# The statistics of chunks 2 and 3 computed, turned, stored and spread at earlier places of one fused attention and feed-forward kernel

## The chip, the cores and the metric
The kernel runs on one core of one Trainium2 chip. The metric is the device time of one execution in microseconds (us); lower is better. The engines of the core named here are TensorE (matrix products and turns), VectorE, ScalarE, GpSimd (three small jobs only) and SyncE (issues nearly all transfers). In the rows they are PE (PEld for its weight loads), DVE, ACT, POOL and SP; a queue of an engine, which issues its transfers, has a q behind the name (SPq).

## What is computed
```python
xn = _layernorm(x, axis=-1)
x = x + attn(xn) + ffn(xn)
# attn: x_norm = layernorm(xn) * gamma + beta; q, k, v = x_norm @ qkv
#       softmax(causal(q k^T * scale)) @ v @ o_proj + xn
# ffn:  h = silu(xn @ w_gate) * (xn @ w_up), of each 4 values the 2 largest kept; h @ w_down
```
x is 2048 rows of 512 values, float32; q, k and v are 512 wide, the hidden layer 2048.

## The kernel before
The 2048 rows are 16 tiles of 128 rows and 4 chunks (0 to 3) of 4 tiles. Every float32 operand of a product is split into a high and a low half, and a product is three matmuls: high by high, high by low, low by high. So a result in PSUM is cast to the high half by ScalarE and then subtracted to the low half by VectorE, which also frees the bank. q and k are never made: the weights are multiplied beforehand, a chunk's z (`zg`) is the transposed chunk by the joint weight, and scores are x by z. In the same way v and the output projection are one weight.

The order of the work is one hand-written list, `steps`. Each engine runs through the same list and emits what it has to do for a step, so a step's place in the list sets its place in the program of each engine, and in SyncE's queue too. An engine takes its instructions strictly in order; what waits holds all that stands behind it. Semaphores order the engines among each other.

The steps that the change moves, for a chunk c:

- `stat[c]` (four) and `x_stats[c]`: VectorE reads the four tiles of x in `xw` (L1510) and joins the sums to mean and variance (L1514).
- `x_rstd[c]`: GpSimd adds and raises to -0.5 (L686, L687, L690).
- `x_scale[c]`: four small VectorE instructions (L1520 to L1523) make the columns of scale and shift, `row_stat`.
- `row_turn[c]`: TensorE turns these columns into rows (L763); `row_copy[c]`: VectorE copies them out of the bank (L1562).
- `row_store[c]`: SyncE stores them to memory (L552); `row_spread[c]`: SyncE waits for that store and loads them back over all 128 partitions, 1 MB, as `spread` (L558).
- `xt_load[c]`: SyncE loads x transposed, 2 transfers of 512 KB (L493). For chunk 2 the destination is where chunk 1's spread lies, so it waits until `xn[1]` has read that.

What uses them: `xh_pre[c][k]` (VectorE, L1541 and L1543) scales the transposed chunk, a quarter k at a time, with `spread` and gamma; `xh[c][k]` rounds it to the high half (ScalarE, L1168) and takes the low half (VectorE, L1565). `z_round[c][k]` are TensorE's products for z (L840, 48 matmuls for a chunk). `xn[c]` (L1549, L1551) applies the first normalization to the same transposed data for the feed-forward part, `xn_store[c]` stores it.

Chunk 0 is attended tile by tile (`head`, `scores`, `attend`, `rows`). Chunks 1 to 3 are done in wide units: `unit[c]` is a list of scores of 128 keys against all 512 rows of the chunk (TensorE L699 to L701, ScalarE's copy L1202, VectorE's maximum L1436 to L1448); then the maximum over the partitions (GpSimd, L693), the softmax in parts (`shift`, `exp_wide`, `split`, `meet`) and the rows. `v[c]` are the four products of V (L699 to L701), their bank is needed again by z of the next chunk. In unit lists of chunk 1, `v[1]` and then z of chunk 2 follow the units; in those of chunk 2, z of chunk 3 follows them. `block_sum` makes four sums of blocks for the feed-forward part and stores them.

The list around the change, before:
```python
between = {3: [*z_round[1][1:4], *z[1]]}
steps += [*u[0:2], ("rows_store", OLD - 1, 0), *stat[2], x_stats[2], x_rstd[2], xn[1][0], x_scale[2], xn[1][1], xn_store[1], xt_load[2], u[2],
          row_turn[2], row_copy[2], row_store[2], u[3], row_spread[2], ...
```
SyncE's waits for these steps:
```python
elif n == 2: sp.wait_ge(xn_ready[1], 2)          # xt_load
else:        sp.wait_ge(stats_ready, NCH)        # xt_load of chunk 3
sp.wait_ge(row_stat_stored, 16 * n)              # row_spread
if n == 3: sp.wait_ge(sums_turned, 1)            # row_spread of chunk 3, over chunk 1's maxima and sums
```

Of the kernel before, what the change touches and what calls it, by code (L numbers as in the profile page):

```python
# [28 lines left out]
def attention_ffn(nc, x, x_t, qkv_t, o_proj, gamma, beta, w_units, w_down, out):  # L29
# [3 lines left out]
    NCH = S // W  # L33
    TC = W // P
# [21 lines left out]
    def fills(kind, n):  # L56
        return [(kind, n, k) for k in range(KT)]
# [4 lines left out]
    xh_pre, xh, z, z_round, v = ([fills(kind, c) for c in range(NCH)] for kind in ("xh_pre", "xh", "z", "z_round", "v"))  # L62
    x_stats, x_rstd, x_scale, row_turn, row_copy, xw_load, row_store, row_spread, xt_load, xn_store = (
        [(kind, c, 0) for c in range(NCH)] for kind in ("x_stats", "x_rstd", "x_scale", "row_turn", "row_copy", "xw_load", "row_store",
                                                        "row_spread", "xt_load", "xn_store"))
    stat = [fills("stat", c) for c in range(NCH)]
    xn = [fills("xn", c)[0:2] for c in range(NCH)]
# [3 lines left out]
    steps = [step for k in range(3) for step in (hi[0][k], hi[1][k], lo[0][k], lo[1][k], qk_round[k])]  # L71
# [6 lines left out]
    steps += [*vo, *stat[1][0:2], *z[0], *stat[1][2:4], x_stats[1], x_rstd[1], xw_load[3], v[0][0],  # L78
              ("scores", 0, 0), exp[0], x_scale[1], row_copy[1], v[0][1], row_turn[1], row_store[1], row_spread[1]]
    before = {3: [z_round[1][0]]}  # L80
    between = {3: [*z_round[1][1:4], *z[1]]}
    beside = {0: [v[0][2]],
              1: [xh_pre[1][0], v[0][3], xh[1][0]],
              2: [xh_pre[1][1], xh_pre[1][2], xh[1][1], xh_pre[1][3], xh[1][2], xh[1][3]]}

# [1 line left out]
    OLD = TC * WIDE[0]  # L87
# [15 lines left out]
    def wide_parts(c):  # L103

        own = TC * c
        return [(0,), (1,), *((u, u + 1) for u in range(2, own + TC, 2))]
# [5 lines left out]
    def softmax(c, after, behind):  # L112

        last = len(wide_parts(c)) - 1
        order = [shift[c][0], exp_wide[c][0], *after.get(-1, []), shift[c][1], split[c][0], *after.get(0, []), shift[c][2], exp_wide[c][1]]
        for j in range(1, last + 1):
            if j == 3:
                order += meet[c][0:3]
            order += [*exp_wide[c][j + 1:j + 2], split[c][j], *after.get(j, []), *shift[c][j + 2:j + 3], *behind.get(j, []), *(meet[c][j:j + 1] if j >= 3 else [])]
        return order  # L120

    rows_of = {c: [[("rows", n, 0), ("rows_store", n, 0)] for n in range(TC * c, TC * (c + 1))] for c in WIDE}
    u = unit[1]
    steps += [*u[0:2], ("rows_store", OLD - 1, 0), *stat[2], x_stats[2], x_rstd[2], xn[1][0], x_scale[2], xn[1][1], xn_store[1], xt_load[2], u[2],
              row_turn[2], row_copy[2], row_store[2], u[3], row_spread[2], *u[4:6], xh_pre[2][0], u[6], xh_pre[2][1], u[7], ("max_fold", 1, 0), ("max_all", 1, 0),
              ("rows_load", OLD + 1, 0), xh[2][0], v[1][0], xh_pre[2][2], xh[2][1], v[1][1], xh_pre[2][3], xh[2][2], v[1][2], xh[2][3], v[1][3], *z_round[2]]
    steps += softmax(1, {}, {2: [*z[2], *xn[0], xn_store[0]], 4: [("block_sum", 0, 0)]})
    steps += [("sum_turn", 1, 0), *rows_of[1][0], *rows_of[1][1], ("rows_load", OLD + 2, 0), ("rows_load", OLD + 3, 0), *stat[3], x_stats[3], x_rstd[3], xt_load[3]]
    u = unit[2]
    steps += [*u[0:3], *rows_of[1][2], x_scale[3], *rows_of[1][3], ("rows_load", OLD + 4, 0), ("rows_load", OLD + 5, 0), u[3],  # L130
              row_turn[3], row_copy[3], row_store[3], row_spread[3], xn[2][0],
              *u[4:6], xn[2][1], xn_store[2], u[6], xh_pre[3][0], u[7], xh_pre[3][1], xh[3][0], u[8], xh_pre[3][2], xh[3][1], u[9],
              xh_pre[3][3], xh[3][2], *u[10:], ("max_fold", 2, 0), ("max_all", 2, 0), xh[3][3], *z_round[3], *z[3][0:2]]
    steps += softmax(2, {-1: [z[3][2]], 0: [z[3][3]], 1: v[2][0:2], 2: v[2][2:4]}, {4: [xn[3][0]], 5: [xn[3][1], xn_store[3]]})
# [1 line left out]
    u = unit[3]  # L136
# [60 lines left out]
    with ExitStack() as ctx:  # L197
        def sem(name):
            return ctx.enter_context(nc.semaphore(name))
# [4 lines left out]
        def at(name, offset, shape, dt):  # L204
            return nc.alloc_sbuf_tensor_at(name, shape, dt, offset=base + offset)
# [8 lines left out]
        def products_ahead(no):  # L214
# [10 lines left out]
                  for c, pair in enumerate(((112, 116), (208, 212), (24, 28), (120, 124)))]  # L225
# [18 lines left out]
                           for name, cols, dt in (("own_raw", OWN_W + P, F32), ("own_lo", OWN_W, F32R)))  # L244
# [4 lines left out]
        sum_pair, max_all = ({c: at(f"{name}{c}", o[c - WIDE[0]] * KB, shape, F32) for c in WIDE}  # L249
                             for name, o, shape in (("sum_pair", (88, 136, 168), [P, 2, W]), ("max_all", (94, 92, 172), [P, W])))  # L250
# [83 lines left out]
        max_ready, exp_ready, group_attended, rows_ready = sem("max_ready"), sem("exp_ready"), sem("group_attended"), sem("rows_ready")  # L334
# [361 lines left out]
        def _(pe):  # L696
# [51 lines left out]
            def row_bank_free(no):  # L748

                if no < TURN_RING:  # L750
                    pe.wait_ge(prod_free, 2 * KT)

            def turn_rows(n):

                c = 0 if n == 1 else n
                no = turn_no["row_turn", n]
                if no >= TURN_RING:
                    pe.wait_ge(turn_free, no - TURN_RING + 1)
                row_bank_free(no)
                if n == NCH - 1:  # L760
                    pe.wait_ge(rows_ready, TC * (n - 1))
                pe.wait_ge(scale_ready, n + 1)
                pe.transpose(turn_bank[no % TURN_RING][0:(n + 1 - c) * 4 * TC, 0:P], row_stat[:, c:n + 1, :, :, :].rearrange("p c v t o -> p (c v t o)"),  # L763
                             ident[:]).then_inc(turn_full, 1)
# [139 lines left out]
            for kind, n, k in steps:  # L904
# [4 lines left out]
                elif kind == "z_round":  # L909
                    z_round(n, k)  # L910
                elif kind == "row_turn":
                    turn_rows(n)
                elif kind == "x_turn":

# [29 lines left out]
                elif kind == "meet":  # L944
                    u = wide_parts(n)[k][-1]
# [957 lines left out]
```

## Time and profile before
| | |
|---|---|
| median of 3 runs | 803.7 us (800.33 to 805.3) |
| the profiled execution | 802.0 us |
| its span, first to last instruction | 800.2 us |
| TensorE busy | 788.8 us (99%) |
| VectorE busy | 610.8 us (76%) |
| ScalarE busy | 319.6 us (40%) |
| GpSimd busy | 18.9 us (2%) |
| mean granted TensorE clock | 0.994 |

The span is the part of the execution that the profile covers, and 1.8 us lie around it. Busy time of TensorE is a modelled figure: matmuls overlap, and one of 512 columns is shown with 0.39 us while the next starts 0.227 us after it. So distances between starts tell more than busy shares. The granted clock is the share of full speed that TensorE was given; full speed is 2.4 GHz, and 0.50 is the lower of its two levels, 1.2 GHz.

### The profile page before, as it was taken

The numbers are of one execution on the slowest core, as the hardware profiler recorded it, in microseconds if no ns is written. First come the engines' busy times: TensorE is split into PE (matmuls) and PEld (weight loads), VectorE is DVE, ScalarE is ACT, GpSimd is POOL, SyncE is SP. The second block draws the span as 40 slices with busy tenths as digits, with TensorE's granted clock in tenths as the row PEclk, the third lists the DMA queues.
The fourth block names the chain that finished last, engine by engine and source line by source line (L and its number), as shares of the span: only waits on it lengthen the run. The fifth ranks groups of instructions, "written<-read, shape, count | busy, mean of one in ns | idle before, by whom it ended". The sixth has DMA issues, their size and how long they took to land.

```text
span 800.2 us, 9296 instructions
## 1 busy us (share of the span) xinstructions
PE 788.8 (99%) x3518; PEld 651.7 (81%) x3518; DVE 610.8 (76%) x964; ACT 319.6 (40%) x514; POOL 18.9 (2%) x26
## 2 busy tenths in 40 slices
PE   9999979989999999999999999999999999999998
PEld 6888858878888888888888888888888888888887
DVE  7978497775824688779989889799559558559786
ACT  5423142124312354564636436364334334335441
POOL 2010110101000000000000000000000000000000
PEclk9999989999999999999999999999999999999999
DMA  9441501730022325587426435497467262261002
GB/s 325 174 169 44 185 0 61 255 106 1 27 79 79 109 102 220 174 325 280 185 73 266 188 79 210 180 348 291 154 214 262 102 235 92 95 236 54 0 1 106
DMA packets 31611, 121.74 MB, mean 152 GB/s; under 512 B 3088, under 2 KB 3664, under 8 KB 29136
## 3 DMA queue, kind: packets, MB, share of 16 engines
q1 hardware_dynamic: 30272, 119.00, 40.4%
q10 hardware_dynamic: 1296, 2.16, 0.8%
q8 instruction: 28, 0.46, 0.2%
q14 instruction: 15, 0.12, 0.0%
HBM read 77.07 MB, written 44.07 MB: 151 GB/s over the span
## 4 chain that ended last, share of the span: by engine, by line
PE 78%; DMA 2%; DVE 1%; issue 0%; ACT 0%; SPq 0%; DVEq 0%
PE bank L960 13%; PE bank L961 13%; PE bank L962 13%; PE bank L1040 7%; PE bank L1042 7%; PE bank L1041 7%; PE bank L701 5%; PE bank L699 5%; PE bank L700 5%; PE bank L840 2%; DMA spread<-row_stats 1%; DMA resid<-rows 0%; DMA row_stats<-rows_turned_t 0%; DVE xh_raw L1541 0%; DVE xh_raw L1543 0%
## 5 line engine op out<-in xcount | busy, mean ns | idle before, releaser
L960 PE MATMUL bank<-X_hi,wset 128*128 128x512 f32 x448 | 174.4, 389 | 0.0
L962 PE MATMUL bank<-X_hi,wset 128*128 128x512 f32 x448 | 174.3, 389 | 0.0
L961 PE MATMUL bank<-X_lo,wset 128*128 128x512 f32 x448 | 174.3, 389 | 0.0
L960 PEld LDWEIGHTS bank<-X_hi,wset 128*128 128x128 f32 x448 | 84.1, 188 | 17.6 <-issue 0.2
L962 PEld LDWEIGHTS bank<-X_hi,wset 128*128 128x128 f32 x448 | 84.1, 188 | 17.5
L961 PEld LDWEIGHTS bank<-X_lo,wset 128*128 128x128 f32 x448 | 84.1, 188 | 17.4
L1040 PE MATMUL bank<-dw,hs_hi 128*128 128x512 f32 x224 | 87.2, 389 | 0.0
L1042 PE MATMUL bank<-dw,hs_lo 128*128 128x512 f32 x224 | 87.1, 389 | 0.0
L1041 PE MATMUL bank<-dw,hs_hi 128*128 128x512 f32 x224 | 87.1, 389 | 0.0
L1674 DVE TENSOR_TENSOR acc<-bank,acc 128x512 f32<-128x512 f32 x59 | 40.1, 687 | 40.0 <-PE bank L1042 39.6
L699 PE MATMUL bank<-zg,xT 128*128 128x512 f32 (+2 forms) x132 | 49.8, 377 | 0.0
L701 PE MATMUL bank<-zg,xT 128*128 128x512 f32 (+2 forms) x132 | 49.5, 375 | 0.0
L700 PE MATMUL bank<-zg,xT 128*128 128x512 f32 (+2 forms) x132 | 49.4, 375 | 0.0
L1040 PEld LDWEIGHTS bank<-dw,hs_hi 128*128 128x128 f32 x224 | 42.1, 188 | 8.9 <-DVE acc L1674 0.2
L1042 PEld LDWEIGHTS bank<-dw,hs_lo 128*128 128x128 f32 x224 | 42.1, 188 | 8.8
L1041 PEld LDWEIGHTS bank<-dw,hs_hi 128*128 128x128 f32 x224 | 42.0, 188 | 8.7
L699 PE MATMUL bank<-v_hi,wide_hi 128*128 128x512 f32 x126 | 49.0, 389 | 0.0
L700 PE MATMUL bank<-v_lo,wide_hi 128*128 128x512 f32 x126 | 49.0, 389 | 0.0
L840 PE MATMUL bank<-xT,mu_hi 128*128 128x512 f32 x128 | 38.9, 420 | 7.4 <-DVE v_lo L1575 5.0
L1221 ACT COPY g_sum<-bank 128x512 f32<-128x512 f32 x32 | 18.9, 589 | 56.5 <-PE bank L962 56.5
L840 PEld LDWEIGHTS bank<-xT,mu_hi 128*128 128x128 f32 x128 | 25.9, 203 | 14.7 <-DVE v_lo L1575 6.3
L1202 ACT COPY wide_raw<-bank 128x512 f32<-128x512 f32 x20 | 11.8, 588 | 58.6 <-PE bank L701 58.6
(259 smaller groups left out, 1441.7 us busy)
## 6 DMA issues: line engine op xcount, KB each, us to landing
w_operands<-wset SPq DMA_DIRECT2D x8, 3584.0 KB, 13.5
wset<-w_operands SPq DMA_DIRECT2D x8, 3584.0 KB, 12.5
wsum<-w_units SPq DMA_DIRECT2D x28, 256.0 KB, 3.8
dw_raw<-L_ffn_w_down SPq DMA_DIRECT2D x14, 512.0 KB, 5.4
xw<-L_attn_x SPq DMA_DIRECT2D x4, 1024.0 KB, 9.6
xt_raw<-x_t SPq DMA_DIRECT2D x8, 512.0 KB, 7.5
xn_t<-xt_raw SPq DMA_DIRECT2D x8, 512.0 KB, 2.8
acc<-resid SPq DMA_DIRECT2D x2, 2048.0 KB, 9.8
```

Source lines behind the costliest of these rows:

```text
L699: pe.matmul(dst, l_hi, r_hi, start=(n == 0 and flags.get("first", True)), stop=False)
L700: pe.matmul(dst, l_hi, r_lo, start=False, stop=False)
L701: last = pe.matmul(dst, l_lo, r_hi, start=False, stop=(n == len(pairs) - 1 and flags.get("last", True)))
L840: return pe.matmul(product_bank(no)[:], lhs[left][:, q, m * P:(m + 1) * P], rhs[right][:, q, :], start=first, stop=(q == KT - 1 and right ...
L960: pe.matmul(dst[:], u[:, 0, :], x_hi, start=(first and kt == 0), stop=False, skip_group_check=True)
L961: pe.matmul(dst[:], u[:, 0, :], x_lo, start=False, stop=False, skip_group_check=True)
L962: last = pe.matmul(dst[:], u[:, 1, :], x_hi, start=False, stop=(kt == 1), skip_group_check=True)
L1040: pe.matmul(dst, s_hi, d_h, start=(r == 0 and i != ND - 2), stop=False)
L1041: pe.matmul(dst, s_hi, d_l, start=False, stop=False)
L1042: last = pe.matmul(dst, s_lo, d_h, start=False, stop=(r == G - 1 and i != ND - 3))
L1221: nc.scalar.copy(dst[:], src[:]).then_inc(kept[m], 1)
L1674: nc.vector.tensor_tensor(acc[:, tile, :], down_bank(i, t)[:], acc[:, tile, :], ALU.add).then_inc(added, 1)
```

## The change
The statistics of chunk 2 go into the attention of chunk 0: two of them ahead of V's third tile, the other two with the sums and GpSimd's step ahead of z of chunk 1, and the scale behind `z[1]`. Chunk 2's turn, copy, store and spread open the part of chunk 1, ahead of its first wide unit and of the load of x transposed. The whole statistics of chunk 3, which stood behind chunk 1's softmax, with the load of chunk 3's transposed x, go into the first units of chunk 1; its turn, copy and store follow unit 4, and its spread stands behind chunk 1's turned sums, ahead of all stores and loads of rows. The last wait of TensorE for rows ahead of chunk 3's turn is gone. The scalings of chunk 2 (`xh_pre[2]`) and its low halves stand one to two steps earlier among units 5 to 7, and ahead of V.
```diff
-    between = {3: [*z_round[1][1:4], *z[1]]}
-    beside = {0: [v[0][2]],
+    between = {3: [*stat[2][2:4], x_stats[2], x_rstd[2], *z_round[1][1:4], *z[1], x_scale[2]]}
+    beside = {0: [*stat[2][0:2], v[0][2]],
...
-    steps += [*u[0:2], ("rows_store", OLD - 1, 0), *stat[2], x_stats[2], x_rstd[2], xn[1][0], x_scale[2], xn[1][1], xn_store[1], xt_load[2], u[2],
-              row_turn[2], row_copy[2], row_store[2], u[3], row_spread[2], *u[4:6], xh_pre[2][0], u[6], xh_pre[2][1], u[7], ("max_fold", 1, 0), ("max_all", 1, 0),
-              ("rows_load", OLD + 1, 0), xh[2][0], v[1][0], xh_pre[2][2], xh[2][1], v[1][1], xh_pre[2][3], xh[2][2], v[1][2], xh[2][3], v[1][3], *z_round[2]]
+    steps += [row_turn[2], row_copy[2], row_store[2], row_spread[2], *u[0:2], ("rows_store", OLD - 1, 0), *xn[1], xt_load[2], xn_store[1],
+              *stat[3], x_stats[3], x_rstd[3], xt_load[3], *u[2:4], x_scale[3], u[4], row_turn[3], row_copy[3], row_store[3], xh_pre[2][0], u[5],
+              xh_pre[2][1], xh[2][0], u[6], xh_pre[2][2], xh[2][1], u[7], ("max_fold", 1, 0), ("max_all", 1, 0), ("rows_load", OLD + 1, 0),
+              xh_pre[2][3], xh[2][2], v[1][0], xh[2][3], *v[1][1:4], *z_round[2]]
...
-    steps += [("sum_turn", 1, 0), *rows_of[1][0], *rows_of[1][1], ("rows_load", OLD + 2, 0), ("rows_load", OLD + 3, 0), *stat[3], x_stats[3], x_rstd[3], xt_load[3]]
+    steps += [("sum_turn", 1, 0), row_spread[3], *rows_of[1][0], *rows_of[1][1], ("rows_load", OLD + 2, 0), ("rows_load", OLD + 3, 0)]
...
-    steps += [*u[0:3], *rows_of[1][2], x_scale[3], *rows_of[1][3], ("rows_load", OLD + 4, 0), ("rows_load", OLD + 5, 0), u[3],
-              row_turn[3], row_copy[3], row_store[3], row_spread[3], xn[2][0],
+    steps += [*u[0:2], *rows_of[1][2], *rows_of[1][3], ("rows_load", OLD + 4, 0), ("rows_load", OLD + 5, 0), *u[2:4], xn[2][0],
...
-                if n == NCH - 1:
-                    pe.wait_ge(rows_ready, TC * (n - 1))
```
SyncE's queue behind the spread of chunk 1, before. `xn_t` with `xt_raw_0_52` and `_1_53` is chunk 1's normalized store, `xt_raw_0_54` and `_1_55` chunk 2's transposed x, `spread_111` chunk 2's spread.
```order
L565 DMA xn_t<-xt_raw_0_52 128x2x512
L565 DMA xn_t<-xt_raw_1_53 128x2x512
L493 DMA xt_raw_0_54<-x_t 128x2x512
L493 DMA xt_raw_1_55<-x_t 128x2x512
L552 DMA row_stats<-rows_turned_t 16x128
L558 DMA spread_111<-row_stats 128x2048
L565 DMA xn_t<-xt_raw_0_50 128x2x512
```
The same place of SyncE's queue with the change; `xt_raw_0_56` and `_1_57` are chunk 3's.
```order
L552 DMA row_stats<-rows_turned_t 16x128
L558 DMA spread_111<-row_stats 128x2048
L493 DMA xt_raw_0_54<-x_t 128x2x512
L493 DMA xt_raw_1_55<-x_t 128x2x512
L565 DMA xn_t<-xt_raw_0_52 128x2x512
L565 DMA xn_t<-xt_raw_1_53 128x2x512
L493 DMA xt_raw_0_56<-x_t 128x2x512
L493 DMA xt_raw_1_57<-x_t 128x2x512
L552 DMA row_stats<-rows_turned_t 16x128
```
Store and spread of chunk 2 have gone from last to first; chunk 3's transposed x and store have come in.

VectorE from the low half of z of chunk 1 (`zg`) to the maximum of unit 4 (the first with `own_raw_86`), before:
```order
L1575 TENSOR_TENSOR zg<-bank,zg 128x512 x4
L1382 TENSOR_SCALAR rows<-rows,one_rstd,neg_mean_rstd 128x512
L1389 SCALAR_TENSOR_TENSOR rows<-bank,inv_sum,rows 128x512
L1510 BN_STATS stats<-xw_80 128x6 x4
L1514 BN_AGGR mean_var<-stats 128x2 x4
L1549 TENSOR_TENSOR xt_raw_0_52<-xt_raw_0_52,spread_110 128x1024
L1551 TENSOR_TENSOR xt_raw_0_52<-xt_raw_0_52,spread_110 128x1024
L1520 SCALAR_TENSOR_TENSOR row_stat<-mean_var,row_stat 128x4
```
VectorE from the same `zg` with the change (line numbers are 2 lower there):
```order
L1573 TENSOR_TENSOR zg<-bank,zg 128x512 x4
L1518 SCALAR_TENSOR_TENSOR row_stat<-mean_var,row_stat 128x4
L1519 TENSOR_SCALAR one_rstd<-row_stat 128x4
L1520 SCALAR_TENSOR_TENSOR neg_mean_rstd<-mean_var,row_stat 128x4
L1521 SCALAR_TENSOR_TENSOR row_stat<-mean_var,row_stat 128x4
L1380 TENSOR_SCALAR rows<-rows,one_rstd,neg_mean_rstd 128x512
L1387 SCALAR_TENSOR_TENSOR rows<-bank,inv_sum,rows 128x512
L1560 COPY rows_turned_t<-bank 16x128
L1547 TENSOR_TENSOR xt_raw_0_52<-xt_raw_0_52,spread_110 128x1024
```
The scale of chunk 2 has come right behind `zg`, and the copy of the turned rows stands ahead of the normalized copy of chunk 1.

VectorE behind the maximum of unit 4 with the change; before, the first scaling (L1541 there) stood behind the maximum of unit 5.
```order
L1446 TENSOR_TENSOR max_pair_95<-max_pair_95,own_raw_86 128x512
L1560 COPY rows_turned_t<-bank 16x128
L1539 SCALAR_TENSOR_TENSOR xh_raw_60<-xt_raw_0_54,gamma_t,spread_111 128x512
L1541 SCALAR_TENSOR_TENSOR xh_raw_60<-spread_111,gamma_t,xh_raw_60 128x512
L1444 TENSOR_TENSOR own_raw_86<-own_raw_86,causal_t 128x128
```
The copy of chunk 3's turned rows now stands just ahead of chunk 2's first scaling.

## Rows read from the trace of the kernel before

**Rows 1.** Waits of PE: line waited for, us in total, times, longest us
```profile
PE bank L840 <- DVE v_lo L1575: 5.0, 3, 2.3
PE bank L840 <- ACT own_raw L1202: 2.4, 1, 2.4
```
**Rows 2.** Windows: stretch, busy time of each engine, clock, DMA share, GB/s
```profile
61.60:73.00 11.40, 11.40 (x54) 9.40 (x53) 9.18 (x15) 4.91 (x9) 0.00 (x0) 1.00 0.14 48
...
105.20:124.90 19.70, 14.69 (x50) 11.08 (x50) 16.34 (x25) 9.33 (x14) 0.89 (x1) 0.83 0.00 0
172.10:187.70 15.60, 13.16 (x51) 10.36 (x51) 9.79 (x19) 3.60 (x8) 2.19 (x1) 0.89 0.00 0
```
**Rows 3.** Timeline of PE, z of chunk 2: start, length, instruction, idle before
```profile
105.23 0.42 PE L840 MATMUL bank<-xT,mu_hi 128*128 128x512 f32 x1
...
111.96 0.79 PE L840 MATMUL bank<-xT,mu_hi 128*128 128x512 f32 x1 [0.47 <-DVE v_lo L1575]
...
124.86 0.39 PE L699 MATMUL bank<-v_hi,wide_hi 128*128 128x512 f32 x1
```
**Rows 4.** Timeline of PE, first wide unit of chunk 2 and z of chunk 3
```profile
142.91 0.48 PE L699 MATMUL bank<-zg,xT 128*128 128x512 f32 x1
...
172.19 0.90 PE L840 MATMUL bank<-xT,mu_hi 128*128 128x512 f32 x2
175.52 1.22 PE L840 MATMUL bank<-xT,mu_hi 128*128 128x512 f32 x2 [2.43 <-ACT own_raw L1202]
...
187.68 0.39 PE L699 MATMUL bank<-vo_hi,xT 128*128 128x512 f32 x1
```
**Rows 5.** Timeline of SPq, store and spread of chunk 2
```profile
88.43 0.50 SPq L552 DMA_DIRECT2D row_stats<-rows_turned_t  x1
93.85 0.35 SPq L558 DMA_DIRECT2D spread<-row_stats  x1
```
**Rows 6.** Line L552, the three stores of turned statistics
```profile
DMA to landing us min/median/max: 1.6/2.4/5.4
```
**Rows 7.** Timeline of DVE: unit 4, first scaling of chunk 2, last low half of V
```profile
91.02 0.69 DVE L1448 TENSOR_TENSOR max_pair<-max_pair,own_raw 128x512 f32<-128x512 f32 x1
...
98.53 0.75 DVE L1541 SCALAR_TENSOR_TENSOR xh_raw<-xt_raw,gamma_t,spread 128x512 f32<-128x512 f32 x1 [4.96 <-DMA spread<-row_stats]
...
111.22 0.69 DVE L1575 TENSOR_TENSOR v_lo<-bank,v_hi 128x512 fp32r<-128x512 f32 x1
```
**Rows 8.** The chain that ended last, from 60 to 175: start, us, what
```profile
160.37 6.83 DMA spread<-row_stats
```
**Rows 9.** Timeline of DVE: low half of V's third tile, zg, statistics
```profile
50.18 0.69 DVE L1575 TENSOR_TENSOR v_lo<-bank,v_hi 128x512 fp32r<-128x512 f32 x1 [2.16 <-ACT v_hi L1182]
...
71.77 2.73 DVE L1575 TENSOR_TENSOR zg<-bank,zg 128x512 fp32r<-128x512 f32 x4 [1.89 <-ACT zg L1182]
...
76.67 2.46 DVE L1510 BATCH_NORM_STATS2 stats<-xw 128x6 f32<-128x512 f32 x4
```
**Rows 10.** Timeline of POOL, the steps for chunks 1 and 2
```profile
41.76 0.23 POOL L686 TENSOR_SCALAR radicand<-mean_var 128x4 f32<-128x4 f32 x1 [23.67 <-DVE mean_var L1514]
...
79.64 1.11 POOL L686 TENSOR_SCALAR radicand<-mean_var 128x4 f32<-128x4 f32 x1 [35.62 <-DVE mean_var L1514]
...
82.06 1.67 POOL L690 TENSOR_TENSOR row_stat<-radicand,neg_half 128x8 f32<-128x8 f32 x1
```
**Rows 11.** Line L493, the eight loads of x transposed
```profile
DMA to landing us min/median/max: 5.3/7.5/12.8
```
**Rows 12.** Groups of instructions from 100 to 125: busy us, mean ns
```profile
L1182 ACT CAST v_hi<-bank 128x512 fp32r<-128x512 f32 x4 | 2.3, 568 | 0.0
```
**Rows 13.** Timeline of DVE: zg of chunk 2, low half of part 3
```profile
123.64 2.73 DVE L1575 TENSOR_TENSOR zg<-bank,zg 128x512 fp32r<-128x512 f32 x4 [0.85 <-ACT zg L1182]
...
132.34 1.09 DVE L1633 TENSOR_TENSOR own_lo<-own_raw,wide_hi 128x896 fp32r<-128x896 f32 x1
```
**Rows 14.** DMA issues: KB each, median us to landing
```profile
rows<-L_attn_x SPq DMA_DIRECT2D x10, 256.0 KB, 2.7
```

## The prediction

> **What bounds the kernel now.** I read the waits of TensorE first, over the whole span. Beside the start there are two: 5.0 us for the low halves of V and 2.4 us for a ScalarE copy, both at line 840, the products z of a chunk [rows 1]. So TensorE sets the time, and a gain can only come from these two places. The windows around them give their full size, since a slowed clock comes on top of the idle time: from 61.6 to 73.0, where z of chunk 1 lies, 54 matmuls take 11.4 us at clock 1.00; the two others have 0.83 and 0.89 [rows 2]. The timeline of TensorE gives the lengths. 48 full matmuls 0.227 us apart, as they stand at full clock, make an undisturbed z 10.9 us long (the 54 hold the same 48 and some narrow ones, 11.4). **Stall A**, z of chunk 2, starts at 105.23 and is followed by other work at 124.86: 19.6 us, so 8.7 us lost [rows 3]. **Stall B**, z of chunk 3, runs from 172.19 to 187.68: 15.5 us, 4.6 us lost [rows 4]. Together 13.3 us; all else in the rows is TensorE's own work.
>
> Why A: on SyncE's queue the store of chunk 2's turned statistics stands behind two loads of x transposed. It is issued at 88.43, and the spread that needs it at 93.85 [rows 5]: 5.4 us, where these stores took 1.6, 2.4 and 5.4 us [rows 6]. The Trainium skill ("DMA: Bandwidth & Descriptors", section on queues, rings and completion order) says that an engine consumes descriptors of a ring in order; these rows agree. The spread lands at 98.5, ending 5.0 us of idle time on VectorE, and from there VectorE works without a gap of note until the last low half of V at 111.91 [rows 7]; only then does TensorE get its last bank (111.96) [rows 3]. Why B: the chain goes through chunk 3's spread, issued at 160.37, 6.8 us on its way, to the scaling at 167.2 [rows 8].
>
> **The change, part by part.** Nothing is added: the same 8 statistics, turns, stores and spreads, minus one TensorE wait.
>
> (1) Two statistics of chunk 2 go ahead of V's third tile of chunk 0, where VectorE stood idle for 2.16 us; they take 0.65 us each and cost nothing. The other two and the four sums (1.6 us) go where it stood idle for 1.89 us before zg [rows 9]. Hidden, with 0.2 to 0.3 us to spare; uncovered, zg and with it the first wide unit of chunk 1 come up to 1.6 us later.
>
> (2) Chunk 2's scale now waits for GpSimd between zg and the last rows, and TensorE turns it before the first wide unit, at 75.7. Statistics end near 71.5. GpSimd's three steps took 4.1 us from 79.64 to 83.73; with the first two as short as the 0.23 us at 41.76 they make 2.3 [rows 10]: ready at 73.8 or 75.6, the scale 0.3 us later than the end of zg (74.4) or than 75.6. TensorE waits 0 or 0.3 us, against 0.4 us lost at the turn near 84 now. I take no change, between 0.3 gained and 0.3 lost.
> The first step took 1.11 us beside VectorE's normalized copy, which has two operands in SBUF, and 0.23 us at 41.76 [rows 10]. The Trainium skill ("SBUF — State Buffer", section on the two separate sides) has GpSimd and VectorE lock a shared port pair when VectorE has two SBUF inputs. Zg has one in PSUM, so by the rule the short price holds and the sum is 0.3 us better than by the long one; no row here decides it.
>
> (3) Copy, store and spread of chunk 2: rows of tile 3 end near 77.0, the copy at 77.3. Store 1.6 to 2.4 us, spread 4.7 (93.85 to 98.5) to 6.8 us [rows 5 to 8]: in place between 83.8 and 86.7, no longer last.
>
> (4) What is last then? VectorE does chunk 1's normalized copy (4.9 us, now in one piece, to 82.2), then chunk 3's statistics (2.8 us, to 85.1), which hide in its old idle time. x transposed for chunk 2 is loaded from 82.2, landing 5.3 to 7.5 us later, the least and the median of these loads [rows 11]: 87.5 to 89.7. The wide units' maxima keep their place in TensorE's rhythm. The one of unit 4 ends near 91.6 [rows 7]; the copy of chunk 3's statistics behind it takes 0.3 us, so chunk 2's first scaling starts at 91.9 instead of 98.5: 6.6 us earlier. From 98.53 to 111.91 VectorE needs 13.4 us [rows 7]; the maximum of unit 5, done before 98.5 now, comes inside: 0.9 us. VectorE's bound for the end of V's last low half is 91.9 + 14.3 = 106.2.
> TensorE's own bound is later: V's last matmul starts 0.23 us before 105.23 and lasts 0.39, ScalarE's cast takes 0.57, the low half 0.69: 106.7 [rows 3, 7, 12]. The fourth bank of z is wanted at 105.23 + 3 × 0.227 = 105.9, so 0.8 us of stall A stays, and VectorE has 0.5 us to spare. **A gains 8.7 − 0.8 = 7.9 us.** I take it that 0.8 us leaves the clock alone: the 2.4 us wait ahead of 175.52 brought it down, and the 46 matmuls behind it took 12.2 instead of 10.4 us [rows 2, 4]. That price, 1.7 us, is the other bound.
>
> (5) The softmax behind it. VectorE starts the shifts 5.2 us earlier (106.65 for 111.82), TensorE ends z 7.9 us earlier; so what slack it has shrinks by 2.7 us. The tightest place is the low half of part 3: VectorE made it at 132.34 + 1.0 = 133.4, TensorE used it at 124.86 + 48 × 0.227 = 135.7 [rows 3, 13]. Slack 2.4 us, minus 2.7, plus what ScalarE's wait for TensorE before zg gives back: VectorE stood idle for 0.85 us there [rows 13]. About 0.4 us is left. I take no stall; the other bound is 2.7 − 2.4 = 0.3 us, and later parts have more slack.
>
> (6) Stall B. TensorE reaches chunk 2's wide units at 135.0 (142.9 now) and z of chunk 3 at 164.2 [rows 4]. Chunk 3's store was long ago; its spread is issued behind the four block sums and the turned sums, near 135.5, and lands by 142.3 even at 6.8 us [rows 8]. Chunk 3's scaling now goes by VectorE's program order: the second half of chunk 2's copy ends near 156.1, the first scaling at 157.6, with three maxima, two more scalings and one low half the third is done at 163.6, ScalarE's activation at 164.3 and its copies of units 10 and 11 at 164.7 and 165.0. TensorE wants these banks at 164.6 and 164.9. So 0.3 us stays of 4.6. **B gains 4.3 us**, between 2.5 us (VectorE 1.8 us late) and 4.6.
>
> (7) Chunk 3's turn costs TensorE 0.2 us before and after alike. Its old wait for rows held nobody. Behind z of chunk 3 everything hangs on TensorE, which does not wait again [rows 1], and moves as a whole.
>
> **Sum**: 7.9 + 4.3 = 12.2 us. The profiled execution took 802.0 us (span 800.2), which gives 789.8; against the median of the runs, 803.7, it is 791.5. I forecast 790.5.
>
> **The rivals.**
> *The load of x transposed comes late* (0.10). It shares the queue with the spread, 1 MB, just ahead. At 12.8 us, the longest of these loads [rows 11], it lands at 95.0: VectorE starts 3.1 us late, 0.5 of them free; A gains 5.3, with some clock lost 4.5. 794. Against it: the 12.8 us belong to the start, with 16 loads queued.
> *The softmax of chunk 1 becomes the bound* (0.08). If my 0.4 us of slack is 1 to 2 us too high, TensorE waits before part 3, and that much comes back: 792 to 793.
> *Rows stand behind the spread* (0.07). SyncE's queue now holds the 1 MB spread ahead of the stores and loads of rows 4 to 7, and VectorE cannot go on to maxima without rows 6 and 7. They are wanted by 146.5. The store of rows 4 lands with the spread at 142, the load takes 2.7 us more [rows 14], 145 to 146 with rows 7: just hidden. If it is 3 us later, B keeps its stall with the clock: 795.
> *Nothing to be had* (0.04): the banks of V hold z up whatever VectorE does, A keeps its 8.7 us, only B gains: 799. Against it: VectorE, not ScalarE, released every matmul at A.
> *Slower than before* (0.03). The same head of the queue: the spread waits for chunk 1's turned sums, and everything of SyncE behind it waits with it. Each us by which rows 6 land after 147 costs VectorE one and TensorE one; past 159 the whole gain is gone, at 165 it is 808 us. This needs 20 us for a store and a load of 256 KB each, and such a load takes 2.7 [rows 14].
>
> **How the numbers follow.** The forecast has 0.68: 790.5, with its own bounds of 788.5 (no clock, no leftovers) to 793.5 (clock lost at A, B at 2.5). Rivals one to three reach to 795, four to 799. The base itself lies between 800.3 and 805.3. The range 786.5 to 797.5 leaves out rivals four and five and the ends. What a measurement of this kernel can tell from no change is about 1%, 8 us: the forecast and most of rivals one and two are beyond it, 0.80; part of rivals one to three and rival four within, 0.17; slower 0.03.
>
> **What would show it.** Right: z of chunk 2 ends 11.5 to 12 us after it starts, one wait of 0.7 us at its fourth matmul; z of chunk 3 in 11.2 us; clock 1.00 in both; VectorE's wait for the spreads is gone, and the first scaling of chunk 2 starts near 92 right behind the copy. Wrong: a wait of VectorE for x transposed ahead of that scaling; TensorE waiting for a low half before part 3; VectorE idle for rows near 143; or clock below 1.00 at 106 to 110.

## The result and the profile after

The changed kernel takes 789.9 us (median of 4 runs, 789.6 to 790.2), the kernel before, on the same chip, 802.0 (800.3 to 805.3): a ratio of 0.984, 95% interval 0.981 to 0.986. The forecast was 790.5. The profiled execution took 789.8 us (span 788.0), 12.2 us less than that of before, which is the sum worked out above. Two executions far from all others (1610 us, one of 20 of the kernel before in the first group of experiments, and 1129 us, one of 5 of the last experiment) are left out of the ratios and ranges.

TensorE's waits, as in [rows 1]:
```profile
PE bank L897 <- DVE warm L1478: 1.0, 1, 1.0
PE bank L838 <- DVE v_lo L1573: 0.5, 1, 0.5
```
Of the 5.0 us at chunk 2's z, 0.5 is left, and the 2.4 us at chunk 3's z is gone. (The first row is the start of the program and stood in the kernel before too; a third one, 0.2 us, is also at the start, at 13.66.) The windows, as in [rows 2], over z of chunks 1, 2 and 3:
```profile
61.60:73.00 11.40, 11.40 (x54) 9.44 (x53) 10.72 (x22) 4.61 (x8) 0.66 (x3) 1.00 0.15 47
105.50:117.40 11.90, 11.42 (x49) 8.94 (x48) 9.15 (x14) 7.11 (x11) 0.00 (x0) 1.00 0.00 0
164.50:175.50 11.00, 11.00 (x49) 8.94 (x49) 6.82 (x15) 2.55 (x6) 2.20 (x1) 1.00 0.00 0
```
The first number behind the stretch is its length; the clock is the third from the end. It was 0.83 and 0.89 in the two lower ones [rows 2] and is 1.00 in both. The timeline of TensorE has the lengths, against [rows 3, 4]:
```profile
62.22 1.07 PE L838 MATMUL bank<-xT,mu_hi 128*128 128x512 f32 x4
...
105.51 1.08 PE L838 MATMUL bank<-xT,mu_hi 128*128 128x512 f32 x3
107.07 0.50 PE L838 MATMUL bank<-xT,mu_hi 128*128 128x512 f32 x1 [0.48 <-DVE v_lo L1573]
...
117.41 0.39 PE L699 MATMUL bank<-v_hi,wide_hi 128*128 128x512 f32 x1
...
164.50 1.20 PE L838 MATMUL bank<-xT,mu_hi 128*128 128x512 f32 x4
...
175.54 0.39 PE L699 MATMUL bank<-vo_hi,xT 128*128 128x512 f32 x1
```
z of chunk 2 takes 117.41 − 105.51 = 11.90 us instead of 19.63, z of chunk 3 175.54 − 164.50 = 11.04 instead of 15.49. These are 7.73 and 4.45 us. The fourth matmul starts 107.07 − 105.51 = 1.56 us after the first, where 0.68 would be undisturbed; so 0.9 us is lost there, though the row says 0.48: it counts from the modelled end of the matmul ahead.

The whole from TensorE's starts: z of chunk 1 began at 62.22, 0.60 us later than the 61.62 of before; from there to z of chunk 2 0.32 us less; A 7.73; from its end to z of chunk 3 0.24 less (47.09 against 47.33); B 4.45. 0.32 + 7.73 + 0.24 + 4.45 − 0.60 = 12.14. Behind z of chunk 3 both spans have 612.5 us left. The 0.60 at the head is no cost of the change: the first 48 matmuls begin at 4.21 in both traces, the next ones at 15.90 before and at 16.50 now, behind that 0.2 us wait for a ScalarE copy, and the first moved instruction runs at 48.54. In another profiled execution of the same changed kernel z of chunk 1 began at 61.83.

The timeline of VectorE: the statistics with the sums and zg, chunk 2's first scaling, V's last low half, the low half of part 3, and the rows of tile 6.
```profile
70.40 1.27 DVE L1508 BATCH_NORM_STATS2 stats<-xw 128x6 f32<-128x512 f32 x2
71.70 0.38 DVE L1512 BATCH_NORM_AGGREGATE mean_var<-stats 128x2 f32<-128x6 f32 x4
72.38 2.73 DVE L1573 TENSOR_TENSOR zg<-bank,zg 128x512 fp32r<-128x512 f32 x4 [0.29 <-ACT zg L1180]
...
91.83 0.27 DVE L1560 COPY rows_turned_t<-bank 16x128 f32<-16x128 f32 x1
92.03 0.73 DVE L1539 SCALAR_TENSOR_TENSOR xh_raw<-xt_raw,gamma_t,spread 128x512 f32<-128x512 f32 x1
...
106.33 0.69 DVE L1573 TENSOR_TENSOR v_lo<-bank,v_hi 128x512 fp32r<-128x512 f32 x1 [0.29 <-ACT v_hi L1180]
...
126.28 1.09 DVE L1631 TENSOR_TENSOR own_lo<-own_raw,wide_hi 128x896 fp32r<-128x896 f32 x1
...
145.63 0.55 DVE L1380 TENSOR_SCALAR rows<-rows,one_rstd,neg_mean_rstd 128x512 f32<-128x512 f32 x1 [6.42 <-DMA rows<-L_attn_x]
```
What to see: VectorE still waits for ScalarE ahead of zg, so the statistics cost nothing; the first scaling stands at 92.03 right behind the copy, with no wait for a transfer; V's last low half waits 0.29 us for ScalarE's cast, so VectorE has 0.29 us to spare there. That the first scaling waits for no transfer does not say how near one was; the landings are read below. A wait of 6.4 us for rows has appeared; what it costs is settled by experiments below. GpSimd's steps for chunk 2, around the start of zg (72.38):
```profile
72.18 0.23 POOL L686 TENSOR_SCALAR radicand<-mean_var 128x4 f32<-128x4 f32 x1 [27.56 <-DVE mean_var L1512]
72.48 0.19 POOL L687 TENSOR_SCALAR radicand<-mean_var 128x4 f32<-128x4 f32 x1
72.76 1.67 POOL L690 TENSOR_TENSOR row_stat<-radicand,neg_half 128x8 f32<-128x8 f32 x1
```
And SyncE's queue, against [rows 5]: store and spread of chunk 2, the loads of its transposed x, and the spread of chunk 3.
```profile
77.59 0.32 SPq L552 DMA_DIRECT2D row_stats<-rows_turned_t  x1
78.95 0.32 SPq L558 DMA_DIRECT2D spread<-row_stats  x1
82.38 0.96 SPq L493 DMA_DIRECT2D xt_raw<-x_t  x2
...
135.79 0.32 SPq L558 DMA_DIRECT2D spread<-row_stats  x1
```
The store took 1.4 us to the spread's issue, where it took 5.4 behind the two loads. Chunk 2's spread landed 4.6 us after its issue, at 83.6. VectorE's first scaling waits for both loads of transposed x; the second one:
```profile
L493 SPq DMA_DIRECT2D xt_raw<-x_t x1: 531/531/531, 82.8 to 82.8; - x1
DMA to landing us min/median/max: 8.5/8.5/8.5
```
It was in place at 82.8 + 8.5 = 91.3, and the scaling began at 92.03: 0.7 us of slack, and not the 2.2 or more that the sum had (87.5 to 89.7). In the other traces of kernels with these two transfers in the same place the second load landed 6.4 to 8.3 us after its issue.

### The profile page after: what moved, and what is told of

Its sections match the earlier page's. It is cut to its first block, busy times and chain, and to the rows that moved or that the text cites. A ratio compares the mean times of both kernels' runs of the same rounds, so it can differ in the third digit from the quotient of the medians.

```text
span 788.0 us, 9292 instructions
## 1 busy us (share of the span) xinstructions
PE 783.7 (99%) x3518; PEld 649.1 (82%) x3518; DVE 610.8 (78%) x964; ACT 318.9 (40%) x514; POOL 16.7 (2%) x26
## 4 chain that ended last, share of the span: by engine, by line
PE 98%; DMA 1%; SPq 0%; ACT 0%; DVE 0%; issue 0%
PE bank L960 13%; PE bank L958 13%; PE bank L959 13%; PE bank L701 10%; PE bank L699 10%; PE bank L700 10%; PE bank L1038 7%; PE bank L838 7%; PE bank L1040 7%; PE bank L1039 7%; DMA raw<-L_attn_qkv 1%; SPq L483 0%; PE bank L709 0%; PE bank L804 0%; PE bank L771 0%; PE bank L1051 0%
## 5 line engine op out<-in xcount | busy, mean ns | idle before, releaser
L838 PE MATMUL bank<-xT,mu_hi 128*128 128x512 f32 x128 | 35.2, 393 | 0.5 <-DVE v_lo L1573 0.5
L1677 DVE TENSOR_TENSOR beats_a<-mag 128x1024 bf16<-128x1024 f32 x13 | 15.9, 1225 | 23.2 <-ACT mag L1223 23.2
## 6 DMA issues: line engine op xcount, KB each, us to landing
wset<-w_operands SPq DMA_DIRECT2D x8, 3584.0 KB, 12.2
```

Source lines behind the costliest of these rows:

```text
L838: return pe.matmul(product_bank(no)[:], lhs[left][:, q, m * P:(m + 1) * P], rhs[right][:, q, :], start=first, stop=(q == KT - 1 and right ...
```

## The experiments

All compare with the kernel before on the same chip, whose median was 801.2 to 801.7 us in them; two kernels compared with each other to tenths of a us must come from the same comparison. The first question was whether the two halves of the change are two separate stalls.

### Chunk 2 alone
The statistics of chunk 3, its turn, store and spread at their old places, with TensorE's old wait.
```diff
-              *stat[3], x_stats[3], x_rstd[3], xt_load[3], *u[2:4], x_scale[3], u[4], row_turn[3], row_copy[3], row_store[3], xh_pre[2][0], u[5],
+              *u[2:5], xh_pre[2][0], u[5],
...
-    steps += [("sum_turn", 1, 0), row_spread[3], *rows_of[1][0], ...]
+    steps += [("sum_turn", 1, 0), *rows_of[1][0], ..., *stat[3], x_stats[3], x_rstd[3], xt_load[3]]
```


> Only chunk 2's steps are moved; chunk 3's stay at their old places, with TensorE's wait for rows. Theory (two stalls, each with its own chain): z of chunk 2 is as short as with the change (11.9 us from 19.6), z of chunk 3 keeps its 15.5 us; the time is 802.0 - 7.7 - 0.0 = 794.3 us, ratio 0.990. Rival (the second stall is a consequence of the first): z of chunk 3 is short here too, and the time is that of the whole change, 790.

Measured: 794.3 us, ratio 0.992 (0.989 to 0.996). TensorE's waits:
```profile
PE bank L841 <- ACT own_raw L1203: 4.2, 3, 2.4
PE bank L900 <- DVE warm L1481: 1.0, 1, 1.0
PE bank L841 <- DVE v_lo L1576: 0.6, 1, 0.6
```
z of chunk 2 took 11.88 us, as in the changed kernel, and stall B stands: the time is the theory's 794.3. In the profiled execution, the slowest of the five (797.2; three took 794.0 to 794.3), B is even larger. From the end of the scores ahead, 164.2, to other work at 182.93 are 18.7 us, 3.2 more than before, with three waits; the store of chunk 3's turned statistics took 4.7 us there, for 2.4. Ahead of chunk 3's first scaling VectorE waits:
```profile
161.32 0.75 DVE L1542 SCALAR_TENSOR_TENSOR xh_raw<-xt_raw,gamma_t,spread 128x512 f32<-128x512 f32 x1 [5.30 <-DMA spread<-row_stats]
```

### Chunk 3 alone
Chunk 2 as before; chunk 3's statistics among units 6 and 7, its turn, copy and store behind V, its spread first behind the turned sums.
```diff
-              row_turn[2], row_copy[2], row_store[2], u[3], row_spread[2], *u[4:6], xh_pre[2][0], u[6], xh_pre[2][1], u[7], ...
+              row_turn[2], row_copy[2], row_store[2], u[3], row_spread[2], *u[4:6], *stat[3], x_stats[3], x_rstd[3], xt_load[3],
+              xh_pre[2][0], u[6], xh_pre[2][1], x_scale[3], u[7], ... v[1][3], row_turn[3], row_copy[3], row_store[3], *z_round[2]]
```


> Only chunk 3's steps are moved: statistics into the wait for chunk 2's spread, turn behind V, spread behind the turned sums. Theory: z of chunk 2 stays near 19.6 us, 0.3 to 0.6 more for the scale and copy in VectorE's chain; z of chunk 3 falls from 15.5 to 11 us; 802.0 - 4.4 + 0.4 = 798.0 us, ratio 0.995. Rival (the stalls are one): no gain, or all of it.

Measured: 797.7 us, ratio 0.996 (0.993 to 0.998). z of chunk 2 has its waits of before (2.47, 2.21 and 0.46 us), z of chunk 3 takes 11.03 us; the theory's 798.0 held. Against the median 801.6 of this comparison chunk 3 alone gains 3.9 us and chunk 2 alone 7.3, together 11.2, where both at once give 12.1. The difference of 0.9 us is inside the intervals of the ratios (some 3 us each way for the one, 2 for the other): the stalls are separate, and neither gain needs the other. Two smaller parts of the change were never varied alone: that chunk 2's scalings stand one to two steps earlier among the units, and that TensorE's wait for rows is gone.

### Chunk 2's store and spread behind its transposed load
```diff
-    steps += [row_turn[2], row_copy[2], row_store[2], row_spread[2], *u[0:2], ("rows_store", OLD - 1, 0), *xn[1], xt_load[2], xn_store[1],
+    steps += [row_turn[2], row_copy[2], *u[0:2], ("rows_store", OLD - 1, 0), *xn[1], xt_load[2], row_store[2], row_spread[2], xn_store[1],
```


> The change, with chunk 2's store and spread issued behind the load of x transposed again; nothing else moves. Theory (the place in SyncE's queue counts): store issued near 83.4 waits behind 1 MB as before, 5.4 us, spread from 88.8, 4.7 us: the first scaling at 93.5 instead of 92.0, z of chunk 2 1.2 us longer, 791.1 us; up to 3 us more if the spread takes 6.8. Rival (the earlier statistics alone did it): no wait for the spread, 789.9.

Measured: 793.7 us, ratio 0.991 (0.987 to 0.995); 2.6 us above the point expected, inside its upper bound. The queue and VectorE:
```profile
83.27 0.50 SPq L552 DMA_DIRECT2D row_stats<-rows_turned_t  x1
88.40 0.34 SPq L558 DMA_DIRECT2D spread<-row_stats  x1
```
```profile
94.74 0.75 DVE L1539 SCALAR_TENSOR_TENSOR xh_raw<-xt_raw,gamma_t,spread 128x512 f32<-128x512 f32 x1 [2.71 <-DMA spread<-row_stats]
```
The store again takes 5.1 us behind the two loads, though the turned rows were ready at 77.5. So it is its place in the queue that makes it late, not when the statistics were made. The 2.6 us beyond the point expected have two parts: the spread took 6.2 us and not 4.7, so the first scaling came at 94.74 and not at 93.5, and the clock fell, for which the point had nothing. VectorE is 2.7 us late, and TensorE waits 1.45 and 0.69 us, but z of chunk 2 takes 15.8 us (from 105.45, where V's matmuls end, to 121.28), 3.9 more than in the changed kernel:
```profile
106.00:108.00 2.00, 0.47 (x1) 0.19 (x1) 2.00 (x4) 1.85 (x4) 0.00 (x0) 1.00 0.00 0
108.00:110.00 2.00, 1.59 (x3) 0.88 (x4) 2.00 (x5) 0.00 (x1) 0.00 (x0) 0.82 0.00 0
110.00:112.00 2.00, 2.00 (x6) 1.60 (x5) 1.68 (x4) 1.78 (x3) 0.00 (x0) 0.50 0.00 0
112.00:114.00 2.00, 2.00 (x8) 1.56 (x8) 1.47 (x3) 0.83 (x1) 0.00 (x0) 0.83 0.00 0
```
The granted clock goes to 0.50, the level of 1.2 GHz, behind these two waits; VectorE's lateness beyond its slack, 2.71 − 0.29 = 2.4 us, leaves 1.5 of the 3.9 to it.

### The queue alone, in the kernel before
Statistics at their old place; chunk 2's store and spread ahead of its transposed load.
```diff
-xn[1][1], xn_store[1], xt_load[2], u[2],
-              row_turn[2], row_copy[2], row_store[2], u[3], row_spread[2], *u[4:6],
+xn[1][1], xn_store[1], u[2],
+              row_turn[2], row_copy[2], row_store[2], row_spread[2], xt_load[2], u[3], *u[4:6],
```


> The kernel before, with only chunk 2's store and spread issued ahead of the load of x transposed. Theory (two orders to mend, statistics and queue): the spread lands near 93, the load now behind it near 94 to 97, the first scaling at 94 to 97 instead of 98.5: z of chunk 2 2 to 4 us shorter, with less lost to the clock 798 to 800 us. Rival (the queue was the whole cause): all of the 7.7 us, 794.

Measured: 800.0 us, ratio 0.998 (0.995 to 1.000), no difference beyond the uncertainty; the theory's upper end, and the rival (794) is out. The profiled execution was the fastest of the ten, 796.9 us.
```profile
97.84 0.75 DVE L1541 SCALAR_TENSOR_TENSOR xh_raw<-xt_raw,gamma_t,spread 128x512 f32<-128x512 f32 x1 [4.07 <-DMA xt_raw<-x_t]
```
Another transfer stands where the spread stood: the first scaling is at 97.8 instead of 98.5, and what it waits for is x transposed, issued at 90.1 instead of 87.0. In this execution z of chunk 2 took 17.75 us, 1.9 less than before, and z of chunk 3 12.2, 3.3 less, with chunk 3's steps unmoved. With the experiment before this one it says that both are needed: early statistics, so that the spread can go first, and the spread first.

### Two and six more instructions on VectorE ahead of chunk 2's first scaling
The first scaling is repeated 2 or 6 times (the same values), 0.76 to 0.79 us from start to start: they delay the scaling by 1.6 us (92.06 to 93.62) and 4.7 us (91.90 to 96.61). The edit for two:
```diff
+                    if n == 2 and k == 0:
+                        for _ in range(2):
+                            done = step(nc.vector.scalar_tensor_tensor(out=part, in0=src, scalar=gain, in1=scale_row, op0=ALU.mult, op1=ALU.mult))
+                            dve.wait_ge(vec_step, done)
```


> The change with two more VectorE instructions (the first scaling's multiplication repeated, 0.75 us each and their waits, 1.6 us) ahead of chunk 2's first scaling. VectorE has 0.3 us of slack there. Theory (short waits leave the clock alone): z of chunk 2 longer by 1.3 us, clock 1.00, 791.2 us. Rival (a 1.8 us wait already lowers the clock): up to 1.7 us more, 793.

> The same with six more instructions, 4.8 us. Theory: 4.5 us of waits come back at z of chunk 2 and the clock falls as before, another 2 to 4 us: 796.5 to 798.5. Rival (idle time only, the clock costs nothing of note): 794.4.

Measured: 791.3 us (0.987, 0.985 to 0.989) with two, 796.0 us (0.993, 0.991 to 0.995) with six. With two, z of chunk 2 took 13.1 us, 1.2 more than in the changed kernel: 1.56 minus the 0.29 of slack that its trace shows. The clock stayed at 1.00 in every window, and the theory held. With six it took 17.8 us, 5.9 more:
```profile
108.92 0.77 PE L838 MATMUL bank<-xT,mu_hi 128*128 128x512 f32 x1 [3.38 <-DVE v_lo L1577]
110.09 1.39 PE L838 MATMUL bank<-xT,mu_hi 128*128 128x512 f32 x2 [0.40 <-DVE v_lo L1577]
```
```profile
106.00:108.00 2.00, 0.00 (x0) 0.00 (x0) 1.97 (x3) 0.45 (x1) 1.73 (x1) 0.97 0.00 0
108.00:110.00 2.00, 0.77 (x1) 0.29 (x1) 2.00 (x5) 1.72 (x4) 0.00 (x0) 0.50 0.00 0
110.00:112.00 2.00, 1.91 (x4) 1.19 (x5) 2.00 (x5) 0.14 (x1) 0.00 (x0) 0.50 0.00 0
112.00:114.00 2.00, 2.00 (x6) 1.53 (x5) 1.68 (x4) 1.65 (x3) 0.00 (x0) 0.50 0.00 0
```
VectorE's last low half of V ends 4.3 us later against the start of z than in the changed kernel; that leaves 1.6 us to the clock, less than the 2 to 4 of the theory, and the time lies 0.5 below its range. The rival, 794.4, is out. So at stall A a late VectorE is paid one for one while TensorE's wait is short, and with 1.5 to 1.6 us on top in these two traces where the clock fell. In the kernel before the fourth matmul of z of chunk 2 started 6.73 us after the first for an undisturbed 0.68 [rows 3], 6.05 us late, and the 45 from there on took 12.90 us for 10.2: 6.05 + 2.7 is why 5.0 us of waits cost 8.7.

### What is left of A: the last bank's products last
In z of chunks 2 and 3, the products of the fourth bank come behind those of the other three, instead of each of the three kinds over all banks.
```diff
+                if n >= 2 and q == 0:
+                    for some in (range(KT - 1), range(KT - 1, KT)):
+                        for m in some:
+                            ...
+                            part("z", n, m, q, lhs, 0, rhs, 0)
+                        for m in some:
+                            part("z", n, m, q, lhs, 1, rhs, 0)
+                        pe.wait_ge(xh_ready, KT * n + q + 1)
+                        for m in some:
+                            part("z", n, m, q, lhs, 0, rhs, 1)
+                    return
```


> The change, and in the first round of z of chunks 2 and 3 TensorE does all nine matmuls of the first three banks ahead of the three of the fourth. Theory (what is left of stall A is only the fourth bank's release, 1.0 us late): the fourth bank is wanted 1.4 us later, the wait goes, z of chunk 2 10.9 to 11.0 us, 788.9 us. Rival (another bank or half comes late next, or the order costs as much elsewhere): 789.9.

Measured: 789.3 us, ratio 0.985 (0.983 to 0.987). z of chunk 2: 105.62 to 116.77, 11.15 us without a wait, so 0.75 of the 1.0 us lost in the changed kernel is back. But z of chunk 3 took 11.27 instead of 11.04. The time lies between the theory (788.9) and the rival (789.9).

### The wait for rows: chunk 3's spread behind the loads of rows
```diff
-    steps += [("sum_turn", 1, 0), row_spread[3], *rows_of[1][0], *rows_of[1][1], ("rows_load", OLD + 2, 0), ("rows_load", OLD + 3, 0)]
+    steps += [("sum_turn", 1, 0), *rows_of[1][0], *rows_of[1][1], ("rows_load", OLD + 2, 0), ("rows_load", OLD + 3, 0), row_spread[3]]
```


> The change with chunk 3's spread issued behind the stores and loads of rows 4 to 7, not ahead. VectorE's wait of 6.4 us for rows shrinks to about 3 us. Theory (that wait is hidden, and the spread has 7 us to spare even so): z of chunk 3 stays 11.0 us, 789.9 within 0.3. Rival (the wait was worth something): 0.5 us or more faster; other side: the spread comes too late, slower by 1 to 3 us.

Measured: 789.6 us, ratio 0.985 (0.983 to 0.987). VectorE has the rows of tile 6 at 142.14 instead of 145.63, and z of chunk 3 takes 11.04 us as in the changed kernel: the 6.4 us wait costs nothing in the changed kernel, as the theory had it.

### Both, and the changed kernel again


> The changed kernel with both small edits together: the products of z of chunks 2 and 3 for their last bank come last, and chunk 3's spread stands behind the loads of rows. Theory: the first edit gives back the 0.5 us wait of chunk 2's z and leaves the rest, the second moves a wait that nobody stands behind; together 789.2 to 789.6 us beside 789.6 to 789.9 for the changed kernel in the same comparison, z of chunk 2 in 11.2 us. Rival: the two are worth their apparent gains each (0.6 and 0.4 us) because both ends were real, 788.9.

> The changed kernel itself, beside the two others on the same chip. Both theories: 789.6 to 789.9 us; it is the base for differences of a few tenths.

Measured side by side: 788.9 us (788.8 to 789.1) with both edits, 789.6 us (789.5 to 789.8) for the changed kernel. It is the best of all: ratio to before 0.984 (0.983 to 0.986), and 0.66 us faster than the changed kernel. The theory (789.2 to 789.6) missed, and the rival's number came. But in the traces, both against the changed kernel's of this comparison, the whole gain is z of chunk 2, 11.14 us for 11.90; z of chunk 3 took 11.01 for 11.03. What the second edit adds is that the first one's gain is kept there. (The edits alone were not measured beside these two, so their tenths can't be set against the 0.66.) VectorE, in the kernel with the last bank late alone:
```profile
146.55 0.55 DVE L1393 TENSOR_SCALAR rows<-rows,one_rstd,neg_mean_rstd 128x512 f32<-128x512 f32 x1 [7.89 <-DMA rows<-L_attn_x]
...
152.68 1.22 DVE L1450 TENSOR_TENSOR max_pair<-max_pair,wide_raw 128x1024 f32<-128x1024 f32 x1
```
In the changed kernel the same maximum has idle time before it, that is, slack behind the rows:
```profile
152.70 1.23 DVE L1437 TENSOR_TENSOR max_pair<-max_pair,wide_raw 128x1024 f32<-128x1024 f32 x1 [0.86 <-ACT wide_raw L1200]
```
And with both edits:
```profile
151.75 1.23 DVE L1450 TENSOR_TENSOR max_pair<-max_pair,wide_raw 128x1024 f32<-128x1024 f32 x1 [1.82 <-ACT wide_raw L1213]
```
The rows' wait was hidden with 0.86 us to spare. In the first edit's run TensorE was 0.55 us earlier, and the rows landed 0.9 us later (146.55 for 145.63): the slack was gone, and z of chunk 3 paid 0.23 us. That the late rows were due to the edit is not shown: in the changed kernel's second trace they came at 144.41, so their landing varies by more than 0.9 us. With both edits 0.25 us is left of stall A and 0.1 of B.

### The load of x transposed one place later
The store of chunk 1's normalized rows (1 MB) ahead of chunk 2's transposed load.
```diff
-    steps += [row_turn[2], row_copy[2], row_store[2], row_spread[2], *u[0:2], ("rows_store", OLD - 1, 0), *xn[1], xt_load[2], xn_store[1],
+    steps += [row_turn[2], row_copy[2], row_store[2], row_spread[2], *u[0:2], ("rows_store", OLD - 1, 0), *xn[1], xn_store[1], xt_load[2],
```


> The changed kernel, but the store of chunk 1's normalized rows (2 x 512 KB) stands ahead of the load of chunk 2's transposed x on SyncE's queue. In the changed kernel the load was issued at 82.4 and the first scaling of chunk 2 began at 92.0, right behind the copy ahead of it, without a wait for the load. Theory: the slack of the load is real but small. It is issued about 1 us later and shares the engines with 1 MB more ahead of it, some 3 us more; it lands 92 to 94. If by 92, 789.9 us; if at 94, VectorE waits 2 us, 0.5 of them free, z of chunk 2 has a wait of 1.5 to 2 us more with some clock lost behind it, 792.5. I take 791.5. Rival: the load had several us of slack and nothing changes, 789.7 to 790.0 with no wait ahead of the scaling.

Measured: 789.6 us, the same as the changed kernel beside it (ratio to before 0.985, 0.983 to 0.987). My 791.5 missed and the rival's time came. The queue and VectorE, and the landing of the second load of chunk 2's transposed x:
```profile
80.03 2.77 SPq L565 DMA_DIRECT2D xn_t<-xt_raw  x2
82.84 3.70 SPq L493 DMA_DIRECT2D xt_raw<-x_t  x4
```
```profile
91.88 0.27 DVE L1560 COPY rows_turned_t<-bank 16x128 f32<-16x128 f32 x1
92.08 0.73 DVE L1539 SCALAR_TENSOR_TENSOR xh_raw<-xt_raw,gamma_t,spread 128x512 f32<-128x512 f32 x1
```
```profile
L493 SPq DMA_DIRECT2D xt_raw<-x_t x1: 1281/1281/1281, 83.4 to 83.4; - x1
DMA to landing us min/median/max: 8.5/8.5/8.5
```
Half of the store goes at 80.0 already, when the first half of the normalized copy is there, so the loads are issued only 0.5 to 0.6 us later. The second one landed at 83.4 + 8.5 = 91.9, and the scaling began at 92.08. So the rival's reason, several us of slack, is refuted: the load came in with 0.1 to 0.2 us to spare. The theory's "if by 92, 789.9 us" is what happened; what it had wrong was the landing at 92 to 94. What a later load would cost was not measured.

## Why the prediction was right, point by point

**What bounds the kernel.** Right: the two stalls are separate (7.3 us with chunk 2 alone, 3.9 with chunk 3 alone, 12 with both), and they were all there was.

**(1) The statistics.** Hidden, as said; 0.29 us to spare ahead of zg, for 0.2 to 0.3.

**(2) GpSimd and the turn.** GpSimd's first step took 0.23 us, begun while VectorE was still idle ahead of zg (72.18 to 72.41), and the second 0.19 us, wholly beside zg; beside the normalized copy they took 1.11 [rows 10] and 1.15. That is the short price. The Trainium skill ("SBUF — State Buffer", section on the two separate sides) has GpSimd shut out by a VectorE instruction with two SBUF inputs; zg has one of its two in PSUM, and the 0.19 us of the second step agree. I had taken no change; from z of chunk 1 to z of chunk 2 TensorE needed 0.32 us less, and chunk 3's turn (some 0.2 us) has come into this stretch.

**(3) The spread in place early.** Right, and it is the step that carries A: with the spread behind the load again, 3.9 us of z of chunk 2 are lost. It landed at 83.6, for 83.8 to 86.7.

**(4) Stall A.** 7.9 us forecast, 7.73 measured. The first scaling came at 92.03 for 91.9, V's last low half ended at 107.0 for 106.7 (0.28 of it because all stood later). Left over: 1.0 us for 0.8. VectorE had 0.29 us to spare for 0.5: one half of a scaling (L1541 at 101.50) took 1.42 us for the usual 0.75 while GpSimd took the maximum over the partitions (100.94 to 103.13); it did so in each trace with the change looked at, and no run tests the cause. The clock stayed up, as taken. One step was right by a margin smaller than reckoned: x transposed was to land at 87.5 to 89.7 and landed at 91.3, so 0.7 us of slack was left where the sum had 2.2 or more. The rival that it comes late was nearer than its 0.10 and its argument (only the loads at the start are slow) make it; that it did not cost anything in this execution is in part luck.

**(5) The softmax.** No wait, as taken. VectorE ended the low half of part 3 at 126.28 + 1.09 = 127.4, TensorE wanted it at 117.41 + 48 × 0.227 = 128.3: 0.9 us of slack, where I had 0.4.

**(6) Stall B.** 4.3 forecast, 4.45 measured: 0.1 us stays of 4.6 for 0.3. The rival that rows stand behind the spread was close: the wait that it names came, 6.4 us long, tile 6 at 145.6 for "145 to 146", with 0.86 us to spare. So "VectorE idle for rows near 143", named as a sign of being wrong, did appear (139.2 to 145.6), and the stall went all the same: the sign was badly chosen, since the idle time itself tells nothing without the slack behind it. A rows load 0.9 us later used that slack up in one run.

**(7) and the sum.** 12.2 us forecast, 12.14 in the trace; A and B by themselves 12.18. That the whole agrees to a tenth is luck: 0.56 us gained between the stalls, which the sum put at nothing, and 0.60 us of scatter at the start, ahead of all that was moved, cancel. The rivals: x transposed late did not come, by 0.7 us, nor did the softmax bound, by 0.9; that no gain is to be had at A is refuted by chunk 2 alone.

**Where my numbers fell short** was behind the prediction. I priced a late VectorE at A without the clock (793.7 for 791.1 with the spread behind the load), although I had named this bound myself, and the spread at its shortest; the fall of the clock with six more instructions I priced too high (2 to 4 us for 1.6). Of the load of x transposed I reckoned the landing too early in the forecast and too late, by some tenths, in the experiment with the store first.

## What to carry to other kernels

When a stall hangs on a transfer, list what is ahead of it in its queue and what will be last once it is moved: here early statistics alone left 3.9 us of what A can give, queue order alone gained nothing that can be told, and only both removed it. Measure a TensorE stall by the distance of starts around it, since the waits shown leave out the modelled ends and a clock that falls behind them. A long wait of an engine with slack behind it costs nothing until something else moves by more than that slack; read the next idle time behind it to see how much there is. And where no wait is shown, look up when the transfer landed: the load of x transposed had 0.7 us left in one trace and 0.1 to 0.2 in another, and neither shows a wait.

## What was not expected of the hardware

- Waits of 1.45 and 0.69 us of TensorE, one close behind the other, were followed by a clock of 0.82, 0.50 and 0.83 over 6 us (the spread behind the load), while waits of 0.23 and 0.70 us (two more instructions) and of 0.48 us left it at 1.00. I had expected only the 2.4 us kind to do it.
- The scatter from run to run goes with stall B. Kernels that keep it: before 798.5 to 805.5 us, the queue alone 796.9 to 803.9, chunk 2 alone 794.0 to 797.2. Kernels without it, though the clock falls at A in all three: chunk 3 alone 797.1 to 798.7, the spread behind the load 793.0 to 795.4, six more instructions 795.8 to 796.5. The changed kernel went from 789.6 to 790.2. The traces of the first three have z of chunk 3 in 15.5, 12.2 and 18.7 us, where VectorE waited 3.27, 1.54 and 5.30 us for the same spread; chunk 3's store took 2.4, 2.3 and 4.7 us to land, the spread 6.1 to 6.8. So it is likely that transfers landing at different times there make the scatter; with one trace of each kernel it is not shown.
- In one profiled execution (the load one place later) the granted clock stands at 0.95 in every window, though its matmuls are 0.227 us apart and its time is that of the others. Here the figure over the whole span said nothing of the work; in the other traces a fall inside one stretch went with matmuls further apart.
- The store of chunk 2's turned statistics took 5.1 and 5.4 us behind two loads of 512 KB, and 1.4 us with the queue free.
